# Sixteen products of value and output weights, moved from the loop over head pairs into the first stage

## What is computed

```python
x = x + _layernorm(_L0_attn_ref(_layernorm(x), ...))     # 32 heads, latent ranks 192 (q) and 64 (kv)
x = x + _layernorm(_L0_ffn_ref(_layernorm(x), ...))      # gated, hidden 1376
# inside the attention
kv = _rmsnorm(compressed, kv_a_ln_w) @ Wkv_b             # per head 128 columns of keys, 128 of values
o = jnp.einsum('bhqk,bhkd->bhqd', probs, v)
return o.transpose(0, 2, 1, 3).reshape(b, s, H * VD) @ Wo
```

## Time and profile before

| | us |
|---|---|
| median of 3 runs (653.73 to 654.58) | 654.0 |
| profiled execution, first to last instruction | 652.1 |
| first stage, to the first exponential | 47.0 |
| first pair, to the product of pair 0 at k = 8, and on to that of pair 1 | 66.0 and 91.7 |
| product of pair 15 at k = 8 | 448.7 |
| last attention output scaled | 467.1 |

### The profile page before, as it was taken

How to read it: one execution, slowest core, us unless ns; L and a number is a source line. 1 busy time by engine, 2 the same in 40 slices (tenths; PEclk the granted TensorE clock), 3 DMA queues, 4 the chain that set the end, 5 groups by cost and what they waited for, 6 DMA issues and landing times.

```text
span 652.1 us, 12397 instructions
## 1 busy us (share of the span) xinstructions
PE 607.9 (93%) x3432; PEld 448.6 (69%) x3432; DVE 529.2 (81%) x1292; ACT 412.8 (63%) x1157; POOL 166.0 (25%) x137
## 2 busy tenths in 40 slices
PE   5778999999999999999999999999999878789996
PEld 4666667767777776677677777766787656666664
DVE  4987788888888888888888888889877888886456
ACT  4455777878777777778787777777733333155343
POOL 2011222122213212221222132121043333125520
PEclk9998999999999999999999999999999998979999
DMA  8000211201202202112012022022760000001003
GB/s 320 16 1 1 82 39 43 80 25 56 80 0 80 65 15 80 36 44 80 19 61 80 0 80 64 17 93 80 234 235 1 0 1 1 28 2 49 0 16 114
DMA packets 13862, 37.80 MB, mean 58 GB/s; under 512 B 1328, under 2 KB 1584, under 8 KB 13584
## 3 DMA queue, kind: packets, MB, share of 16 engines
q1 hardware_dynamic: 13840, 37.53, 17.3%
HBM read 31.24 MB, written 6.29 MB: 58 GB/s over the span
## 4 chain that ended last, share of the span: by engine, by line
PE 71%; DVE 18%; ACT 4%; issue 3%; DMA 3%; SPq 0%; DVEq 0%; ACTq 0%
PE bank L1002 13%; PE bank L1014 12%; PE bank L961 11%; PE bank L962 11%; PE bank L963 11%; DVE dot L833 6%; PE bank L1032 2%; PE bank L1024 2%; PE bank L971 2%; PE bank L985 2%; PE bank L984 2%; DMA x<-x 2%; PE bank L1181 2%; DVE st L809 2%; DVE ss L635 1%
## 5 line engine op out<-in xcount | busy, mean ns | idle before, releaser
L367 ACT ACTIVATE pr<-ss,small 128x128 f32<-128x128 f32 (+3 forms) x256 | 143.2, 559 | 41.4 <-DVE small L635 40.8
L375 ACT ACTIVATE pt<-bank 128x128 f32<-128x128 f32 (+3 forms) x256 | 110.9, 433 | 61.3 <-PE bank L1002 61.1
L635 DVE CUSTOM_DVE_ANT_0 ss<-bank,cst 128x128 f32<-128x128 f32 (+3 forms) x256 | 123.3, 486 | 14.0 <-PE bank L963 9.6
L1002 PE MATMUL bank<-ident,pr 128*128 128x128 f32 x640 | 119.0, 284 | 3.1 <-ACT pr L367 2.9
L1002 PEld LDWEIGHTS bank<-ident,pr 128*128 128x128 f32 x640 | 75.6, 142 | 66.6 <-ACT pr L367 34.0
L284 POOL TENSOR_TENSOR qrot<-qrot,qswp 64x512 f32<-64x512 f32 x64 | 82.8, 1294 | 138.5 <-DVE qrot L621 138.5
L961 PE MATMUL bank<-kt_hi,qt_hi 128*128 128x128 f32 (+3 forms) x256 | 101.0, 394 | 3.6 <-DVE qt_lo L625 2.7
L1014 PE MATMUL bank<-pt,kvn 128*64 128x256 f32 (+3 forms) x512 | 86.2, 448 | 0.7 <-ACT pt L375 0.7
L963 PE MATMUL bank<-kt_hi,qt_lo 128*128 128x128 f32 (+3 forms) x256 | 83.2, 325 | 0.0
L962 PE MATMUL bank<-kt_lo,qt_hi 128*128 128x128 f32 (+3 forms) x256 | 83.0, 324 | 0.0
L625 DVE TENSOR_TENSOR qt_lo<-qrot,qt_hi 128x512 fp32r<-128x512 f32 x64 | 60.3, 942 | 24.7 <-ACT qt_hi L357 24.5
(11 more groups left out here) (168 smaller groups left out, 1179.7 us busy)
## 6 DMA issues: line engine op xcount, KB each, us to landing
sv<-sv SPq DMA_DIRECT2D x16, 576.0 KB, 3.7
sq<-sq SPq DMA_DIRECT2D x16, 448.0 KB, 3.5
wvo_scratch<-vs SPq DMA_DIRECT2D x16, 256.0 KB, 2.1
wv_raw<-wvo_scratch SPq DMA_DIRECT2D x8, 512.0 KB, 4.2
xa<-x SPq DMA_DIRECT2D x8, 256.0 KB, 5.5
x<-x SPq DMA_DIRECT2D x1, 2048.0 KB, 10.9
out<-yo SPq DMA_DIRECT2D x8, 256.0 KB, 2.0
w<-w SPq DMA_DIRECT2D x1, 1376.0 KB, 14.1
```

Source lines behind the costliest of these rows:

```text
L367: nc.scalar.activation(pr[:, k % 4, 0:n], ss[:, k % 2, 0:n], ACT.Exp, bias=negmax[:, k % 8:k % 8 + 1], scale=-1.0, accum_out=rsum[:, k:k + ...
L375: nc.scalar.activation(pt[:, b, h, 0:i + 1, i * P:(i + 1) * P], bank[2 + k % 2][:, 0:(i + 1) * P].rearrange("p (j q) -> p j q", q=P), ACT. ...
L635: nc.vector.tensor_tensor_reduce(out=ss[:, k % 2, 0:n], in0=bank[k % 2][:, 0:n], in1=mask[:, SEQ - n:SEQ], scale=-SCALE, scalar=3.4e38, op ...
L1002: last = nc.tensor.transpose(bank[2 + k % 2][:, j * P:(j + 1) * P], pr[:, k % 4, j * P:(j + 1) * P], ident[:, :])
```

## The change

All sixteen products leave the loop. Fourteen go into steps t = 3 to 10 of the first stage, by a table `EARLY` of (step, bank): two in each of t = 3 to 7 into banks 6 and 7, one in t = 8 (bank 0), two in t = 9 (banks 1 and 0) and one in t = 10 (bank 1). The last two are made in pair 0, at k = 5 and k = 8, into bank 5. ACT copies each out at the end of its own step t (`move_absorbed`), behind `deviation(t + 1)` and ahead of `query_hi`; the last two at k = 6 and k = 9 of pair 0. There are three buffers of `sv` (in space that the second half of `pt` uses later) and two of `vs`. SP's list has all loads and stores of the products ahead of the loop that loads `sq`, with `sq` of pair 1 after the fourth store; `cst` is loaded between the first and the second `sv`. PE waits for copies before it reuses banks: before the first query, before the first two scores, and between products of one bank.

```diff
+SV_BUFS = 3
+EARLY = ((3, 6), (3, 7), (4, 6), (4, 7), (5, 6), (5, 7), (6, 6), (6, 7), (7, 6), (7, 7), (8, 0), (9, 1), (9, 0), (10, 1))
...
-            sp.dma_start(cst[:, :], cst_d).then_inc(f.cst_in, 16)
-            sp.dma_start(sv[:, :], sv_d[0]).then_inc(a.sv_in, 16)
-            with nc.sync.Fori(0, PAIRS - 1) as p:
+            for j in range(SV_BUFS):
+                if j == 1:
+                    sp.dma_start(cst[:, :], cst_d).then_inc(f.cst_in, 16)
+                sp.dma_start(sv[:, j, :], sv_d[j]).then_inc(sv_in[j], 16)
+            for j in range(PAIRS):
+                if j == 4:
+                    sp.wait_ge(a.wq_split, 1)
+                    sp.dma_start(sq[:, :], sq_d[1]).then_inc(a.sq_in, 16)
+                if j + SV_BUFS < PAIRS:
+                    sp.wait_ge(a.wvo_made, j + 1)
+                    sp.dma_start(sv[:, j % SV_BUFS, :], sv_d[j + SV_BUFS]).then_inc(sv_in[j % SV_BUFS], 16)
+                sp.wait_ge(a.wvo_moved, j + 1)
+                sp.dma_start(wvo_d[j], vs[:, j % 2, :]).then_inc(wvo_out[j % 2], 16)
+            with nc.sync.Fori(1, PAIRS - 1) as p:
                 sp.wait_ge(a.wq_split, p + 1)
                 sp.dma_start(sq[:, :], sq_d[bass.ds(p + 1, 1)].rearrange("a p n -> p (a n)")).then_inc(a.sq_in, 16)
-                sp.wait_ge(a.wvo_made, p + 1)
-                sp.dma_start(sv[:, :], sv_d[bass.ds(p + 1, 1)].rearrange("a p n -> p (a n)")).then_inc(a.sv_in, 16)
-                sp.wait_ge(a.wvo_moved, p + 1)
-                sp.dma_start(wvo_d[bass.ds(p, 1)].rearrange("a p n -> p (a n)"), vs[:, :]).then_inc(a.wvo_out, 16)
...
-                    if k == 9:
-                        act.wait_ge(a.wvo_made, p + 1)
-                        if not first:
-                            act.wait_ge(a.wvo_out, 16 * p)
-                        nc.scalar.activation(vs[:, :], bank[XB][:, :], ACT.Copy).then_inc(a.wvo_moved, 1)
+                    if first and k in (6, 9):
+                        move_absorbed(PAIRS - 2 + k // 9, XB)
+
+            def move_absorbed(j, at):
+                act.wait_ge(a.wvo_made, j + 1)
+                if j >= 2:
+                    act.wait_ge(wvo_out[j % 2], 16 * (j // 2))
+                nc.scalar.activation(vs[:, j % 2, :], bank[at][:, :], ACT.Copy).then_inc(a.wvo_moved, 1)
...
                 if t == 2:
                     weights_hi(0, first=True)
+                for j, (at, b) in enumerate(EARLY):
+                    if at == t:
+                        move_absorbed(j, b)
                 if t in (TB + 1, TB + 3):
...
-                    if k == 8:
-                        if first:
-                            pe.wait_ge(a.wq_split, p + 2)
-                        else:
-                            pe.wait_ge(a.r_moved, 2 * p)
-                        absorb_output(p)
+                    if first and k == 5:
+                        pe.wait_ge(a.wq_split, p + 2)
+                        absorb_output(PAIRS - 2, XB)
+                    if first and k == 8:
+                        pe.wait_ge(a.wvo_moved, PAIRS - 1)
+                        absorb_output(PAIRS - 1, XB)
...
                 if t == TB:
                     pe.wait_ge(f.qk_split, QB)
+                    pe.wait_ge(a.wvo_moved, 10)
...
+                for j, (at, b) in enumerate(EARLY):
+                    if at == t:
+                        if b < 2:
+                            pe.wait_ge(f.xt_split, TB - 1 + b)
+                        earlier = [i for i in range(j) if EARLY[i][1] == b]
+                        if earlier:
+                            pe.wait_ge(a.wvo_moved, earlier[-1] + 1)
+                        absorb_output(j, b)
                 if t in (TB + 2, TB + 3):
+                    pe.wait_ge(a.wvo_moved, (13, 14)[t - TB - 2])
                     scores(t - TB - 2, t - TB - 2, 0, first=True)
```

More of the change, by code:

```diff
@@ L103, in build @@
     kvn = att.take("kvn", [P, TB, P])
-    sv = att.take("sv", [P, SV_COLS])
+    vs = att.take("vs", [P, 2, D])
+    att.at += 4 * SV_COLS - 4 * 2 * D
     qt_hi = att.take("qt_hi", [P, BATCH, 2, SEQ], F32R)
@@ L113, in build @@
     rsb = att.take("rsb", [P, SEQ])
-    vs = att.take("vs", [P, D])
-    att.at += 32
+    att.at += 4 * D + 32
     pt = att.take("pt", [P, 2, 2, QB, SEQ])
+    sv = Map(nc, att.at - 4 * 2 * QB * SEQ, att.at).take("sv", [P, SV_BUFS, SV_COLS])
     negmax = small[:, 0:8]
@@ L200, in build @@
     x_in = [nc.alloc_semaphore(f"x_in{t}") for t in range(TB)]
-    a = sems("attention", """s_seen rinv_seen sq_in sv_in wq_made wq_hi_made wq_split q_made q_rotated pe_added qt_hi_made qt_split
+    sv_in = [nc.alloc_semaphore(f"sv_in{j}") for j in range(SV_BUFS)]
+    wvo_out = [nc.alloc_semaphore(f"wvo_out{j}") for j in range(2)]
+    a = sems("attention", """s_seen rinv_seen sq_in wq_made wq_hi_made wq_split q_made q_rotated pe_added qt_hi_made qt_split
         s_made s_masked exp_made p_turned p_moved o_made rinv_made rb_made r_made r_moved o_scaled
-        wvo_made wvo_moved wvo_out""")
+        wvo_made wvo_moved""")
     c = sems("projection", """rstd2_made xn2_made wv_in0 wv_in1 wv_in2 wv_copied wv_hi_made wv_split o_hi_made o_split o_used x1_in w13_in bs_in a13_in
@@ L226, in _ @@
                 sp.dma_start(xa[:, t, :], xb[t]).then_inc(x_in[t], 16)
-            sp.dma_start(cst[:, :], cst_d).then_inc(f.cst_in, 16)
-            sp.dma_start(sv[:, :], sv_d[0]).then_inc(a.sv_in, 16)
-            with nc.sync.Fori(0, PAIRS - 1) as p:
+            for j in range(SV_BUFS):
[12 more added lines that the diff above has]
+            with nc.sync.Fori(1, PAIRS - 1) as p:
                 sp.wait_ge(a.wq_split, p + 1)
                 sp.dma_start(sq[:, :], sq_d[bass.ds(p + 1, 1)].rearrange("a p n -> p (a n)")).then_inc(a.sq_in, 16)
-                sp.wait_ge(a.wvo_made, p + 1)
-                sp.dma_start(sv[:, :], sv_d[bass.ds(p + 1, 1)].rearrange("a p n -> p (a n)")).then_inc(a.sv_in, 16)
-                sp.wait_ge(a.wvo_moved, p + 1)
-                sp.dma_start(wvo_d[bass.ds(p, 1)].rearrange("a p n -> p (a n)"), vs[:, :]).then_inc(a.wvo_out, 16)
             sp.wait_ge(a.q_made, 4 * PAIRS)
+            for n in range(2):
+                sp.wait_ge(wvo_out[n], 16 * (PAIRS // 2))
             for k in range(PAIRS // 2):
-                if k == 4:
-                    sp.wait_ge(a.wvo_moved, PAIRS)
-                    sp.dma_start(wvo_d[PAIRS - 1], vs[:, :]).then_inc(a.wvo_out, 16)
                 if k >= 3:
                     sp.wait_ge(c.wv_split, 2 * (k - 2))
-                if k == PAIRS // 2 - 1:
-                    sp.wait_ge(a.wvo_out, 16 * PAIRS)
                 sp.dma_start(wv_raw[:, k % 3, :, :], wvo_d[2 * k:2 * k + 2].rearrange("a p n -> p a n"))\
@@ L1026, in turn_r, with absorb_output @@
                 last.then_inc(a.r_made, 1)
-            def absorb_output(p):
-                pe.wait_ge(a.sv_in, 16 * (p + 1))
+            def absorb_output(j, at):
+                pe.wait_ge(sv_in[j % SV_BUFS], 16 * (j // SV_BUFS + 1))
+                w = sv[:, j % SV_BUFS, :]
                 for h in range(2):
-                    last = nc.tensor.matmul(bank[XB][RKV * h:RKV * (h + 1), :], sv[:, h * RKV:(h + 1) * RKV],
-                                            sv[:, 2 * RKV + h * D:2 * RKV + (h + 1) * D], start=True, stop=True)
+                    last = nc.tensor.matmul(bank[at][RKV * h:RKV * (h + 1), :], w[:, h * RKV:(h + 1) * RKV],
+                                            w[:, 2 * RKV + h * D:2 * RKV + (h + 1) * D], start=True, stop=True)
                 last.then_inc(a.wvo_made, 1)
@@ L1092, in body @@
                     if k == 11:
-                        pe.wait_ge(a.wvo_moved, p + 1)
+                        if first:
+                            pe.wait_ge(a.wvo_moved, PAIRS)
+                        else:
+                            pe.wait_ge(a.r_moved, 2 * p)
                         turn_r(2 * p)
```

## The result

| | before | after |
|---|---|---|
| median | 653.9 us (4 runs, 652.2 to 654.6) | 665.0 us (4 runs, 662.3 to 665.3) |
| profiled execution | 652.1 | 660.6 |
| first exponential | 46.98 | 59.37 |
| queries of pair 0, then of pair 1 (PE L971, after: L986) | 53.12, 78.49 | 64.87, 91.23 |
| one pair (13 from pair 1 to 14) | 25.67 | 25.39 |

The ratio is 1.0165, with a 95% interval from 1.014 to 1.019: slower by 11 us, where +1.7 was predicted and 659.5 us was the upper end of the range. The matmuls that multiply the query weights ("queries" in the table, `absorb_query`) mark the same point of every pair in both kernels. So the table splits the 8.4 us between the profiled executions: first stage +12.39, pair 0 +0.35, thirteen pairs -3.58, end of the attention 0.0, the wait for the load of `x` behind it -0.72.

What follows compares the result with a forecast made beforehand. PE was taken to set each pair (busy 25.33 of 25.5 us). Terms +6.9, +1.0, -0.5 and -5.7 sum to +1.7, so 652.1 becomes 653.8 profiled; with 1.9 for the median 655.7 us, range 649.0 to 659.5.

Steps and rivals of the forecast that it cites:

- The first stage: Steps 3 to 10, up to the first exponential: copies and products on the chain add 6.9 us (4.9 to 9).
- the loads and stores cost nothing: First-stage DMA: each load lands 0.7 us or more before its product, so the added transfers cost 0.
- Rival C: First stage starved by its DMAs: products from step 4 wait 0.5 us each for loads, some 4 us, 659.5; chance 0.13.
- Rival D: Steps 3 to 6: VectorE leads, copies are hidden, up to 3 us of the first-stage cost vanish, 652.7; chance 0.14.
- Pair 0: First pair of the attention: the product at k = 5 costs its full time, +1.0 us (0.9 to 2.0).
- clock (-0.5): PE's half-clock stretches around the first exponential: half of the first one's loss comes back, -0.5 us (-2.0 to +1.0).
- The loop: Pairs 1 to 14: each gets 0.41 us shorter, held by VectorE's low half behind GpSimd's add; -5.7 us in all.
- Rivals A: Loop: VectorE's low half passes GpSimd's add, each pair gives 0.69 us, pairs of 24.8, 651.7 in all; chance 0.20.
- B (24.4): Loop: PE sets the pair all the same, 14 pairs give 15.4 us, pairs of 24.4, 646.0; chance 0.10.
- Behind the loop: After the last pair: PE's list, not the tile loads, leads to the end of the attention; nothing changes.

Runs made afterwards that it cites:

- late stores: Changed kernel with all loads kept, but the sixteen stores sent after the last product and ACT waiting for none; 665.45 us.
- small add: GpSimd's add of the rotated queries over 1 column instead of 512, in both kernels: 647.1 us in the kernel before, 646.5 us in the changed kernel.

## Why the prediction was wrong

- **The first stage (+6.9 predicted, +12.4 measured).** The step that failed is "the loads and stores cost nothing". It priced a load by its landing when alone and looked whether each load is in time for its product; it never looked at the store, which frees one of only two buffers for a copy that, by the same text, has no slack. The runs showed stores that land after 4.4 us instead of 2.0, four waits of ACT for them, and 6.3 us more at the first exponential than without the loads. The rate (340 GB/s needed, 410 seen) was no evidence of room either. The DMA share, the last figure but one of the windows view, was nearly as high with loads and stores mixed as in the stretch before the first product (0.95 against 1.04), at a lower rate (321 against 412 GB/s):

```profile
10.00:15.00 5.00, 5.00 (x26) 1.00 1.04 412
25.00:30.00 5.00, 4.03 (x24) 1.00 0.95 321
```

  The rest of the sum was right. Without loads, or with late stores, the first exponential came at 53.0 and 52.6, where 53.9 was predicted; from the first squares on the stage got 6.5 us longer, for 6.9. The rest of the way from 53.9 is chance: in these two profiles the stage also started 0.4 and 0.8 earlier (first squares at 14.78 and 14.36, before at 15.20).
- **Rival C** had transfers that starve the stage, at 4 us (6.3 came), but named the load. With two output buffers the store was late first; with six, the load was. **Rival D**, hidden copies, fell: a step grew by both copies, to 4.97 us.
- **Pair 0 (+1.0) and clock (-0.5).** From the first exponential to the queries of pair 0 6.14 us became 5.50, from there to those of pair 1 25.37 became 26.36: -0.64 and +0.99. The two sizes came as put in this execution, in part by luck. PE's granted clock fell to half twice, as in the kernel before (near 58 and 72 us; before near 47 and 61), where half of the first fall was expected to go. And the product at k = 5 held PE for 1.6 us, not 1.0, since it fell into the second stretch at half clock:

```profile
71.43 1.66 PE L1048 MATMUL bank<-sv 128*64 128x512 f32 x4 [1.91 <-DVE w L620]
73.02 0.80 PE L976 MATMUL bank<-ql_hi,w_hi 128*128 128x512 f32 x1
```

  In the second profile the same two stretches were +1.1 and +1.9, and the product took 1.9. That leaves +1.1 for the clock, at the upper end of its range (-2.0 to +1.0). This makes up most of the difference between +8.4 in the first profile and +11.7 in the second; the medians differ by 11.
- **The loop (-5.7 predicted, -3.6 measured).** The mechanism was right, in place and size: the low half 1.44 long (1.4 said), the exponential of k = 15 ready 23.41 us behind the pair's first turn of probabilities (k = 0) in both kernels, pair 15 without gain (last output scaled 54.2 us behind the queries of pair 14 in both). The rule of the Trainium skill ("SBUF — State Buffer", SBUF: two separate sides) that was weighed there, that the one that starts first holds the shared ports for its whole length, agrees with the small add, which took the low half from 1079 to 691 ns. Mis-sized was the slack: 0.41 was taken, 0.28 came. PE turns the last probabilities 0.06 behind ACT as assumed, but these four turns then last 0.47 until the next matmul instead of 0.36 (191.73 to 192.20, against 180.20 to 180.56), for their weights could no longer be loaded ahead (the first load starts with the turn, where it had started 0.23 ahead). I also counted 14 lengths where 13 lie between pairs 1 and 14, and took 25.5 for a pair that the same marks put at 25.67. Rivals A (pairs of 24.8) and B (24.4) fell.
- **Behind the loop** nothing was predicted; -0.7 came in the first profile (the load of `x`), +0.1 in the second.

With the first stage and the loop as measured the sum is 12.4 + 1.0 - 0.5 - 3.6 = +9.3; the two profiled executions were +8.4 and +11.7.

## What to carry to other kernels

When work with its own transfers is moved into a stage, follow each buffer round its whole circle: product, copy, store, free again. If the copy sits on a chain without slack, the store's landing behind the other traffic sets the number of buffers. And before you take work off the busiest engine, ask which other engine's operation ends just behind it; here one VectorE operation held by a GpSimd add, ahead of the masks, kept 0.8 of 1.08 us, and moving that one operation gave 5 to 6 us in the kernel before, with no product moved. When you compare two profiles, first look whether they stand level ahead of the change: here the start of the stage alone differed by up to 1.5 us.

## What the runs showed of the hardware

- A store of 256 KB landed 2.0 us after its issue with the thirteen loads left out, and 4.4 when loads of 576 KB were issued ahead of it on the same queue. The mean rate was then 299 GB/s (10 to 60 us), with a DMA share of 0.92 to 1.02 in the windows from 20 to 45 us; between 10 and 15 us the share was 1.04 at 412 GB/s.
- VectorE's operation with two SBUF inputs took 0.69 us with the small add, and 0.81 to 1.66 when it ran beside GpSimd's add of 1.29, ending 0.54 to 0.56 behind it each time; masks that read PSUM ran at their length beside the add (0.41 and 0.55 above).
- PE's clock stood at 0.68 of full between 35 and 40 us in the profile where PE had waited 1.96 us for a load just before, and at 1.00 in the other profile of the same program, without that wait. The first exponential came 2.8 us later, the end 1.0.
- Two executions of the changed kernel had their half-clock stretches of different length: from the first exponential to the queries of pair 1 one took 31.9 us, the other 34.6, with all pairs behind them equal (25.39 and 25.40).
